# A two-layer audio transformer on one core: norm scaling on GpSimd and ScalarE, a spread-out order in the experts, and a split maximum in the second attention

## The chip, the cores and the metric

The kernel runs on one core of one Trainium2 chip. The metric is device time in microseconds, taken from the chip, of one execution of the whole program. TensorE, VectorE, ScalarE and GpSimd each run their own list of instructions and meet through semaphores; SyncE issues transfers.

## The reference, cut to what matters

A front end turns 16 signals into 16 sequences of 255 tokens with 64 features. Two layers follow, each an attention and a mixture of experts, all with a residual sum and a layer norm in front:

```python
def reference(x, ...):
    h = _L0_tok_ref(x)                                   # 16 x 255 x 64
    h = h + _L0_attn_ref(_layernorm(h), Q, K, VO)        # 8 heads, softmax over 255 keys
    h = h + _L0_ffn_ref(_layernorm(h), ...)              # 16 experts, 2 taken per token, a layer norm of its own
    h = h + _L1_attn_ref(_layernorm(h), ...)             # 8 heads, patch scores and position scores blended
    h = h + _L1_ffn_ref(_layernorm(h), ...)              # 8 experts
    return h

def _layernorm(x, eps=1e-05):
    m = mean(x); v = var(x)
    return (x - m) / sqrt(v + eps)

def _L0_ffn_ref(x, gate_w, gate_b, w1, b1, w2, b2, gamma, beta):
    topk_vals, topk_idx = top_k(x @ gate_w + gate_b, 2)
    topk_w = softmax(topk_vals)
    h = relu(einsum('bsh,ehf->bsef', x, w1) + b1)
    expert_out = einsum('bsef,efh->bseh', h, w2) + b2
    y = x + sum(topk_w * expert_out[topk_idx])
    return layernorm(y) * gamma + beta
```

## The kernel before, in words

**Layout.** Tokens lie 128 to a tile, two tiles to a sequence, 32 tiles of 128 x 64 in `res`, the residual. `x2` holds each normed tile twice side by side, so that its transposes fill 128 rows. The phases run one after the other: front end, first attention (`attention0`, about 127 to 389 us), first experts (`experts0`, 389 to 609), a short preparation, second attention (`attention1`, 644 to 850), second experts to 950. Within a phase the engines' orders are written out by hand; a block of each engine's code calls `slot` or `chunk` in step with the others. `link` waits on VectorE for its own last result.

**Layer norm (`TileNorm`, L500 to L540).** VectorE takes `bn_stats` (L515), `bn_aggr` (L521) and variance plus epsilon (L523). GpSimd raises it to −0.5 (`root`, L528). VectorE subtracts the mean and multiplies (`normed`, L531), `scale_twice` for each tile of a group, writing it twice.

**First attention.** A slot is a quarter of a two-sequence round (two heads pairs), so a sequence has two slots `g`. TensorE: projections (L612, L616), scores L624, the turn of the probabilities L634, outputs' turn L639, outputs L651. VectorE: maxima L787 of the scores, reciprocal L793, copy L799 of the turned probabilities, the residual sum L804, then statistics of the sequence before and, in the other slot, `scale_twice` for the sequence before that. ScalarE: exponentials L722, projections out L714, outputs out L730. GpSimd: weighing L872 (the exponentials times the reciprocals, two per slot), `fetch` L868 of the sequence two ahead between them, and `root`.

**First experts.** Eight chunks of 4 tiles; a chunk has 8 steps `e` of two experts each. TensorE per step: `hidden` L1616 of the next step, `second` L1624 of this one; in steps set by constants also the logits of the next chunk (L1598), the turned columns (L1590), the turned weights (L1606) and the turned sum of the chunk before (L1632). ScalarE: the relu L1695 (two per step), and in single steps `gap` L1679 (the exponential of the difference of the two best logits), the weights out L1685 and columns out L1675. VectorE: per step `scalar_tensor_tensor` L1823 (bias, times the spread weight) and a sum L1801; beside them `best` of the next chunk (L1722 to L1734: bias, `max`, `max_index`, the subtraction L1733, the cast), `places`, `shares` and `spread` (L1739 to L1756), and for the chunk before `finish` (L1765 to L1793: sum, own norm, gain, shift, residual) and `next_norm` (L1760) of the chunk before that. SyncE writes the weights to DRAM (L1891) and reads them back spread over the partitions (L1898), 2 x 4 per chunk. GpSimd: a fetch L1856 and two roots per chunk. The order is set by two places, the constants and the list of what VectorE does in each step:

```python
TURN_SUM, COLUMNS, LOGITS, WEIGHTS = 2, 6, 0, 4
...
extra = [first, ahead[0:2], ahead[2:3] + late[0:1], late[1:3], before[0:2], before[2:3], late[3:5], late[5:7]]
```

**Second attention.** Four units `p` per sequence. TensorE keeps operands in three bf16 parts: `project` L1251, `stack` L1257 gathers them with selector matrices, scores L1263, transposes L1297 of the maximum (as two bf16 parts `mhl`), turned scores L1269, outputs L1279 and the tail of the sequence before (L1312, L1319, L1323). ScalarE: stacks out L1358 and L1360, `high` L1366, outputs L1382, L1387, exponential L1393. VectorE: `maxima` L1418 to L1427 (the reduce L1420, its high part L1426, its remainder L1427), the sum `qm` L1438, the subtraction `remains` L1416 of the projected values in unit p = 0, statistics, `scale_twice`, blends L1450 to L1459. GpSimd: two further parts of the values (L1491, L1493), the pads L1500, the position scores' sum L1505. `stack` at p = 2 waits for those parts of the next sequence (`s_parts`).

## Time and profile before

| | |
|---|---|
| time, median of 3 runs | 949.48 us (949.08 to 949.72) |
| the profiled execution's own time | 951.54 us |
| its span, first to last instruction | 949.7 us |
| mean granted TensorE clock | 0.889 |
| TensorE busy | 696.9 us (73%) |
| VectorE busy | 673.8 us (71%) |
| ScalarE busy | 471.6 us (50%) |
| GpSimd busy | 307.3 us (32%) |

A row of the profile names line, engine and operation, then output and input by name, and how often it ran; behind the bar stand busy time, mean ns of one, and the idle time of the engine just before those instructions with what ended it. PE is TensorE, DVE VectorE, ACT ScalarE, POOL GpSimd, SP SyncE. PEclk, in stretches of the span, is the granted TensorE clock with 1.00 for 2.4 GHz and 0.50 for 1.2 GHz. The profiled execution is a little longer than the median of the runs (951.54 against 949.48 us).

### The profile page before, as it was taken

How to read it: one execution, taken by the hardware profiler on the slowest of the kernel's cores; microseconds unless marked ns; L12 is line 12 of the kernel's file. 1: busy time of each engine (PE TensorE's matmuls, PEld its weight loads, DVE VectorE, ACT ScalarE, POOL GpSimd, SP SyncE). 2: the span in 40 equal slices, each digit the busy share in tenths (PEclk: the TensorE clock that was granted, in tenths of full speed). 3: DMA queues.
4: the chain of work that ended last, by engine and by line, in shares of the span. 5: the costliest groups of instructions: out<-in, count | busy, mean ns of one | idle time of the engine just before them, and what ended most of it. 6: DMA issues, size and time to landing. Idle time of an engine off the chain costs nothing. (4 is left out here: it accounts for less than half of the span.)

```text
span 949.7 us, 16815 instructions
## 1 busy us (share of the span) xinstructions
PE 696.9 (73%) x5015; PEld 379.5 (40%) x5035; DVE 673.8 (71%) x1733; ACT 471.6 (50%) x1173; POOL 307.3 (32%) x310
## 2 busy tenths in 40 slices
PE   0012247899999998499988888376988888867895
PEld 0011124556565565222332322363554444546342
DVE  0289947888888888468777779764788888856353
ACT  0036437767667665055444444133766666632442
POOL 0299325555665656200111001242222222230000
PEclk9996558999999999699887889587999999985798
DMA  0200200000000000143222222000000000000000
GB/s 9 78 0 0 88 1 1 1 1 0 0 0 0 0 0 1 68 134 103 80 80 78 78 80 89 1 1 1 2 1 0 0 0 0 0 1 0 5 19 22
DMA packets 21240, 24.30 MB, mean 26 GB/s; under 512 B 11854, under 2 KB 12110, under 8 KB 20942
## 3 DMA queue, kind: packets, MB, share of 16 engines
q1 hardware_dynamic: 18989, 23.31, 8.1%
q10 hardware_dynamic: 2209, 0.49, 0.2%
q8 instruction: 19, 0.31, 0.1%
q14 instruction: 23, 0.19, 0.1%
HBM read 22.48 MB, written 1.31 MB: 25 GB/s over the span
## 5 line engine op out<-in xcount | busy, mean ns | idle before, releaser
L872 POOL TENSOR_TENSOR big<-big 128x1024 f32<-128x1024 f32 x64 | 121.1, 1893 | 72.2 <-DVE big L793 72.1
L722 ACT ACTIVATE big<-ps,big 128x255 f32<-128x255 f32 x256 | 117.6, 487 | 12.4 <-DVE big L787 7.0
L1695 ACT ACTIVATE big<-ps,b1s 128x512 f32<-128x512 f32 x128 | 80.1, 684 | 61.3 <-PE ps L1616 61.3
L528 POOL TENSOR_TENSOR big<-big 128x2 f32<-128x2 f32 (+1 forms) x48 | 39.5, 826 | 212.0 <-DVE big L523 212.0
L787 DVE TENSOR_REDUCE big<-ps 128x4 f32<-128x1020 f32 x64 | 74.7, 1209 | 23.4 <-PE ps L624 23.4
L799 DVE COPY mid<-ps 128x1024 f32<-128x1024 f32 x64 | 78.2, 1222 | 16.3 <-PE ps L634 10.8
L1624 PE MATMUL ps<-big,w2s 128*64 128x512 f32 x256 | 75.2, 668 | 16.3 <-ACT big L1695 16.2
L1420 DVE TENSOR_REDUCE big<-ps 128x4 f32<-128x1020 f32 x65 | 79.1, 1217 | 7.7 <-PE ps L1263 6.7
L1393 ACT ACTIVATE big<-ps 128x1024 f32<-128x1024 f32 x64 | 66.2, 1034 | 35.0 <-PE ps L1269 35.0
L634 PE MATMUL ps<-cst,big 128*128 128x128 f32 x512 | 67.6, 275 | 19.7 <-DVE mid L799 19.5
L1616 PE MATMUL ps<-big,wall 64*128 64x512 f32 x256 | 81.5, 707 | 0.0
L1823 DVE SCALAR_TENSOR_TENSOR big<-ps,b2s,mid 128x512 f32<-128x512 f32 x64 | 48.0, 751 | 43.0 <-PE ps L1624 21.7
L714 ACT ACTIVATE big<-ps 128x512 f32<-128x512 f32 x64 | 39.4, 616 | 70.9 <-PE ps L612 43.5
L634 PEld LDWEIGHTS ps<-cst,big 128*128 128x128 f32 x512 | 55.8, 141 | 37.7 <-issue 36.3
L651 PE MATMUL ps<-mid,big 128*64 128x256 f32 (+1 forms) x512 | 69.5, 392 | 0.3 <-DVE mid L799 0.3
L1257 PE MATMUL ps<-big,selqk 128*128 128x256 bf16 x396 | 57.2, 283 | 3.5 <-POOL big L1493 2.4
L722 ACT ACTIVATION_READ_ACCUMULATOR big<-ps,big 128x1 f32 x256 | 56.4, 220 | 0.0
L361 PE MATMUL ps<-cst,big 128*128 128x128 f32 x16 | 3.6, 386 | 66.8 <-DVE big L293 66.8
L387 PE MATMUL ps<-cst,big 128*128 128x128 f32 x64 | 15.1, 387 | 49.5 <-DVE big L445 32.9
L531 DVE TENSOR_SCALAR big<-res,big (+1 forms) x64 | 41.7, 693 | 4.8 <-POOL big L528 3.3
L1157 DVE TENSOR_TENSOR big<-big,ps 128x512 f32<-128x512 f32 x32 | 20.6, 684 | 32.6 <-PE ps L1066 21.9
L1257 PEld LDWEIGHTS ps<-big,selqk 128*128 128x128 bf16 x396 | 34.2, 100 | 22.0 <-issue 13.9
(251 smaller groups left out, 1400.1 us busy)
## 6 DMA issues: line engine op xcount, KB each, us to landing
mid<-spread_w SPq DMA_DIRECT2D x128, 128.0 KB, 2.8
mid<-in_split_sel SPq DMA_DIRECT2D x1, 1536.0 KB, 6.1
wall<-in_w SPq DMA_DIRECT2D x1, 1280.0 KB, 7.0
cst<-in_consts SPq DMA_DIRECT2D x1, 666.5 KB, 5.0
mid<-in_w_raw SPq DMA_DIRECT2D x1, 620.0 KB, 6.4
w2s<-in_w SPq DMA_DIRECT2D x1, 512.0 KB, 3.4
out_tokens<-res SPq DMA_DIRECT2D x8, 64.0 KB
out_tokens<-res SPq DMA_DIRECT2D x8, 63.5 KB
```

The costliest lines, as they stand in the source:

```text
L634: last = nc.tensor.transpose(AT[:, j, c, P * tq:P * tq + P], e_sb[r % 4][:, j, tq, P * c:P * c + P], ident)
L651: last = nc.tensor.matmul(O[D * j:D * j + D, par], val[par][0:n, c, D * h:D * h + D], a_sb[r % 4][0:n, j, c], start=(g == 0 and a == 0 and ...
L722: last = nc.scalar.activation(e_sb[r % 4][:, jj, tq, 0:NW], S[:, 2 * (r % 2) + jj, tq, 0:NW], ACT.Exp, scale=-1.0, bias=minus[r % 4][:, jj ...
L787: nc.vector.tensor_reduce(minus[r % 4], S[:, 2 * a:2 * a + 2, :, 0:NW], AX.X, ALU.min).then_inc(s_mx, 1)
L799: nc.vector.tensor_copy(a_sb[r % 4], AT).then_inc(s_at, 1)
L872: nc.gpsimd.tensor_tensor(e_sb[r % 4], e_sb[r % 4], bc(inverse[r % 4].unsqueeze(3), [P, 2, 2, 256]), ALU.mult).then_inc(s_A, 1)
L1257: last = nc.tensor.matmul(out_, selqk[:, 2 * p + n, part], parts[par][:, part], start=(part == 0), stop=(part == 2))
L1393: nc.scalar.activation(e_sb[k % 4], T, ACT.Exp, scale=scale).then_inc(s_E, 1)
L1420: link(nc.vector.tensor_reduce(mx, S[:, :, :, 0:NW], AX.X, ALU.max))
L1616: last = nc.tensor.matmul(H1(e, j), wst[0][half, f:f + P], xc[q][half], start=True, stop=True)
L1624: last = nc.tensor.matmul(Y(e)[D * j:D * j + D], w2s[0][:, 2 * e + j], hid[e % 2][j], start=True, stop=True)
L1695: last = nc.scalar.activation(hid[e % 2][j], H1(e, j), ACT.Relu, bias=b1s[0][:, 2 * e + j:2 * e + j + 1])
```

## The change

It has three parts. In the first attention VectorE's `scale_twice` goes, and GpSimd does the scaling in `normalise`: root, a wait for it, two `tensor_scalar` of 128 x 128. GpSimd's order becomes weigh, weigh, fetch or normalise, with its loop written out.

In the first experts the scalings of the own norm (four of 128 x 64, steps 4 and 5) and of the next one (four of 128 x 128, steps 1 and 2, for the chunk three before) are activations on ScalarE with a scale and a bias; GpSimd makes the bias, minus mean times root, in `root_and_shift`, behind waits of its own. The tile `new` and its sum go. `gap` moves from step 1 to step 3, the turned weights from 4 to 5, the turned sum from 2 to 1; the subtraction stands ahead of `max_index`, which with the cast becomes `which`, two steps later.

In the second attention TensorE's scores of the next unit wait for the reduce alone (`s_max`), the max transposes come behind scores, stack and the turned scores of the unit before, and the exponential one unit later. `mx` is double, VectorE's order is maxima, qm, `max_parts`, and `remains` and the statistics go from p = 0 to p = 1. OT moves to another bank of PSUM.

```diff
+            def root_and_shift(self, pool, i):
+
+                pool.wait_ge(self.s_var, i + 1)
+                nc.gpsimd.tensor_tensor(self.rs, self.var, self.nh, ALU.pow).then_inc(self.s_half_way, 1)
+                pool.wait_ge(self.s_half_way, 2 * i + 1)
+                nc.gpsimd.tensor_tensor(self.shift, self.both[:, :, 0], self.rs, ALU.mult).then_inc(self.s_half_way, 1)
+                pool.wait_ge(self.s_half_way, 2 * i + 2)
+                nc.gpsimd.tensor_tensor(self.shift, self.minus, self.shift, ALU.subtract).then_inc(self.s_rs, 1)
 
...
+                            if not known or b >= 2:
+                                dve.wait_ge(s_nx, b - 1)
                             norm.variance()
-                        if g == 0 and (not known or b >= 2):
-                            tiles = span(2 * (b - 2), 2)
-                            norm.scale_twice(dve, b - 2, x2[:, tiles], res[:, tiles])
                         copy(2 * k + 1, 2 * N + 1)
                         if unit:
                             inverses(2 * k + 3, 2 * N + 3)
...
-                    def slot(j, k, more=True):
-                        N = 2 * QUADS * j + k
-                        par, g = at(k)
-                        b = 2 * j + par
-                        weigh(2 * k, 2 * N)
-                        if g == 0 and more:
-                            fetch(b + 2, par)
-                        weigh(2 * k + 1, 2 * N + 1)
-                        if g == 1 and (not isinstance(j, int) or b >= 1):
-                            norm.root(pool, b - 1)
+                    def normalise(b):
+
+                        norm.root(pool, b)
+                        pool.wait_ge(norm.s_rs, b + 1)
+                        for n in range(2):
+                            t = 2 * b + n
+                            last = nc.gpsimd.tensor_scalar(x2[:, t], bc(res[:, t].unsqueeze(1), [P, 2, D]), norm.both[:, n, 0:1], norm.rs[:, n:n + 1],
+                                                           ALU.subtract, ALU.mult)
+                        last.then_inc(s_nx, 1)
 
                     for b in range(2):
                         fetch(b, b)
                     pool.wait_ge(norm.s_nh, 1)
                     pool.wait_ge(s_pad, 4)
-                    for k in range(2 * QUADS):
-                        slot(0, k)
-                    with pool.Fori(1, B // 2 - 1) as j:
-                        for k in range(2 * QUADS):
-                            slot(j, k)
-                    for k in range(2 * QUADS):
-                        slot(B // 2 - 1, k, False)
-                    norm.root(pool, B - 1)
+                    for b in range(B):
+                        for g in range(QUADS):
+                            for R in (4 * b + 2 * g, 4 * b + 2 * g + 1):
+                                weigh(R, R)
+                            if g == 0 and b + 2 < B:
+                                fetch(b + 2, b % 2)
+                            if g == 1 and b >= 1:
+                                normalise(b - 1)
+                    normalise(B - 1)
...
 
 
                         U = 2 * PAIRS * j + k
@@ -1288,20 +1301,23 @@
                         par, p = at(k)
                         b = 2 * j + par
                         if "unit" in do:
-                            pe.wait_ge(s_mhl, U + 1)
-                            if not known or U >= 1:
-                                pe.wait_ge(s_qm, U)
-                            if p == 0 and (not known or b >= 2):
-                                pe.wait_ge(s_otr, b - 1)
-                            for tq in range(2):
-                                last = nc.tensor.transpose(MT[:, P * tq:P * tq + P], mhl[k % 2][:, tq], ident_b[:])
-                            last.then_inc(s_mtp, 1)
                             pe.wait_ge(s_q, U + 2)
                             pe.wait_ge(s_k, U + 2)
+                            pe.wait_ge(s_max, U + 1)
                             scores(k + 1)
                             if p == 2:
                                 pe.wait_ge(s_parts, b + 2)
                             stack(at(k + 2)[0], at(k + 2)[1])
+                        if "turned" in do and (not known or U >= 1):
+                            pe.wait_ge(s_qm, U)
+                            if not known or U >= 2:
+                                pe.wait_ge(s_E, U - 1)
+                            turned_scores(k - 1)
+                        if "unit" in do:
+                            pe.wait_ge(s_mhl, U + 1)
+                            for tq in range(2):
+                                last = nc.tensor.transpose(MT[:, P * tq:P * tq + P], mhl[k % 2][:, tq], ident_b[:])
...
+                            if p == 3 and (not known or b >= 2):
+                                pe.wait_ge(s_oT, b - 1)
+                                nc.tensor.matmul(Y.rearrange("p t d -> p (t d)"), oT_sb, wps[:], start=True, stop=True).then_inc(s_y, 1)
                             if p == 3 and (not known or 1 <= b <= B):
-                                if "unit" in do:
-                                    pe.wait_ge(s_qm, U + 1)
                                 pe.wait_ge(s_O, QUADS * b)
                                 for tq in range(2):
                                     for g in range(QUADS):
                                         last = nc.tensor.matmul(OT[:, tq, 4 * HS * g:4 * HS * g + 4 * HS], o_sb[(par + 1) % 2][:, g, P * tq:P * tq + P], cmp, start=True, stop=True)
                                 last.then_inc(s_OT, 1)
...
                         if p % 2 == 0 and (not known or b >= 1) and "o" in do:
                             g = p // 2
                             act.wait_ge(s_PV, QUADS * b - 1 + g)
                             if g == 0 and (not known or b >= 3):
                                 act.wait_ge(s_OT, b - 2)
                             nc.scalar.activation(o_sb[(par + 1) % 2][:, g], O[:, g], ACT.Copy).then_inc(s_O, 1)
+                        if "exp" in do and (not known or U >= 1):
+                            act.wait_ge(s_T, U)
+                            if not known or U >= 5:
...
                         dve.wait_ge(s_S, U + 1)
-                        link(nc.vector.tensor_reduce(mx, S[:, :, :, 0:NW], AX.X, ALU.max))
+                        nc.vector.tensor_reduce(mx[k % 2], S[:, :, :, 0:NW], AX.X, ALU.max).then_inc(s_max, 1)
+
+                    def max_parts(U, k):
+                        dve.wait_ge(s_max, U + 1)
                         if not isinstance(U, int) or U >= 2:
                             dve.wait_ge(s_mtp, U - 1)
 
                         m = mhl[k % 2].rearrange("p t (j c) -> p t j c", j=2)[:, :, :, ROWS:ROWS + 2]
-                        mt = mx.rearrange("p j t -> p t j")
...
                         if "unit" in do:
+                            maxima(U + 1, k + 1)
                             dve.wait_ge(s_mtp, U + 1)
                             if not known or U >= 2:
                                 dve.wait_ge(s_T, U - 1)
                             nc.vector.tensor_tensor(qm[k % 2], qs[k % 4], MT, ALU.add).then_inc(s_qm, 1)
-                            maxima(U + 1, k + 1)
-                        if p == 0 and "unit" in do:
+                            max_parts(U + 1, k + 1)
...
+            TURN_SUM, COLUMNS, LOGITS, GAP, WEIGHTS = 1, 6, 0, 3, 5
             pos = [0]
             def take(n, dt=F32):
                 a = big[:, pos[0]:pos[0] + n]
@@ -1556,8 +1568,7 @@
+                    def own_scale(c, tiles):
+                        act.wait_ge(own.s_rs, c + 1)
+                        for t in tiles:
+                            nc.scalar.activation(yy[:, t], yy[:, t], ACT.Identity, scale=own.rs[:, t:t + 1], bias=own.shift[:, t:t + 1]).then_inc(s_sc, 1)
+
+                    def next_scale(c, tiles):
+                        act.wait_ge(norm.s_rs, c + 1)
+                        for t in tiles:
+                            one = slice(TC * c + t, TC * c + t + 1)
+                            nc.scalar.activation(x2[:, one], bc(res[:, one].unsqueeze(2), [P, 1, 2, D]), ACT.Identity,
+                                                 scale=norm.rs[:, t:t + 1], bias=norm.shift[:, t:t + 1]).then_inc(s_nx, 1)
...
-                            if e == LOGITS + 1 and (not known or c < CH - 1):
+                            if e in (1, 2) and c >= 3:
+                                next_scale(c - 3, ((0, 1), (2, 3))[e - 1])
+                            if e == GAP and c < CH - 1:
                                 gap(c + 1)
+                            if e in (4, 5) and c >= 1:
+                                own_scale(c - 1, ((0, 1), (2, 3))[e - 4])
...
-
                         for n in range(TC):
                             last = nc.vector.max(v8[:, n], lg[:, n])
                         link(last)
-                        nc.vector.memset(step[:, 1:2], 0.0)
+                        nc.vector.tensor_tensor(wts[:, 0], v8[:, :, 1], v8[:, :, 0], ALU.subtract).then_inc(s_dv, 1)
+
+                    def which(c):
                         for n in range(TC):
                             last = nc.vector.max_index(i8[:, n], v8[:, n], lg[:, n])
                         link(last)
-                        nc.vector.tensor_tensor(wts[:, 0], v8[:, :, 1], v8[:, :, 0], ALU.subtract).then_inc(s_dv, 1)
                         link(nc.vector.tensor_copy(idx, i8[:, :, 0:2]))
...
                     def next_norm(c):
 
-                        return [lambda: norm.stats(new), norm.variance,
-                                lambda: norm.scale_twice(dve, c, x2[:, span(TC * c, TC)], new)]
+                        def variance():
+                            if c >= 1:
+                                dve.wait_ge(norm.s_rs, c)
+                            norm.variance()
+
+                        return [lambda: norm.stats(res[:, TC * c:TC * c + TC]), variance]
...
-                        def scale():
-                            dve.wait_ge(own.s_rs, c + 1)
-                            for t in range(TC):
-                                last = own.normed(yy[:, t], yy[:, t], t)
-                            link(last)
-
                         def gain():
+                            dve.wait_ge(s_sc, TC * (c + 1))
                             link(nc.vector.tensor_tensor(yy, yy, bc(gb[:, 0].unsqueeze(1), shape), ALU.mult))
 
                         def shift():
                             link(nc.vector.tensor_tensor(yy, yy, bc(gb[:, 1].unsqueeze(1), shape), ALU.add))
 
                         def add():
-                            link(nc.vector.tensor_tensor(new, res[:, tl], yy, ALU.add))
                             nc.vector.tensor_tensor(res[:, tl], res[:, tl], yy, ALU.add).then_inc(s_fin, 1)
                             dve.wait_ge(s_fin, c + 1)
 
-                        return [total, stats, own.variance, scale, gain, shift, add]
...
-                        first = [lambda: best(c + 1)] if not known or c < CH - 1 else none
-                        ahead = combine(c + 1) if not known or c < CH - 1 else none * 3
-                        before = next_norm(c - 2) if not known or c >= 2 else none * 3
-                        extra = [first, ahead[0:2], ahead[2:3] + late[0:1], late[1:3], before[0:2], before[2:3], late[3:5], late[5:7]]
+                        total, stats, variance, gain, shift, add = finish(c - 1) if c >= 1 else [lambda: None] * 6
+                        places, shares, spread = combine(c + 1) if c < CH - 1 else [lambda: None] * 3
+                        next_stats, next_variance = next_norm(c - 2) if c >= 2 else [lambda: None] * 2
+                        first, second = [lambda: best(c + 1), lambda: which(c + 1)] if c < CH - 1 else [lambda: None] * 2
+                        extra = [[first], [total, stats], [variance, second], [places], [shares, spread], [next_stats, next_variance], [gain, shift], [add]]
...
+                    def chunk(c):
+                        if c < CH - 2:
                             fetch(c + 2)
-                        if not known or c >= 2:
-                            norm.root(pool, c - 2)
-                        if not known or c >= 1:
-                            own.root(pool, c - 1)
+                        if c >= 1:
+                            own_root(c - 1)
+                        if c >= 2:
+                            next_root(c - 2)
 
```

## Rows read from the trace of the kernel before

**Rows 1.** Waits of 389 to 609 us (us in total, times, longest).

```profile
PE ps L1624 <- ACT big L1695: 16.2, 8, 3.5
```

**Rows 2.** Timeline, TensorE (start, duration; idle before in brackets).

```profile
411.23 1.08 PE L1624 MATMUL ps<-big,w2s 128*64 128x512 f32 x4 [1.14 <-ACT big L1695]
...
451.81 1.76 PE L1624 MATMUL ps<-big,w2s 128*64 128x512 f32 x4 [1.91 <-ACT big L1695]
```

**Rows 3.** Timeline, first experts, around 477 us.

```profile
476.73 0.21 ACT L1679 ACTIVATE big<-big 128x4 f32<-128x4 f32 x1 [5.75 <-DVE big L1733]
...
477.00 0.75 DVE L1823 SCALAR_TENSOR_TENSOR big<-ps,b2s,mid 128x512 f32<-128x512 f32 x1 [0.22 <-DVE big L1734]
...
478.59 0.16 DVE L1751 TENSOR_TENSOR big<-big 128x4 f32<-128x4 f32 x1
```

**Rows 4.** Windows, TensorE (length, busy, count, PEclk, DMA share, GB/s).

```profile
404.99:588.69 183.70, 167.50 (x665) 0.90 0.30 93
412.00:414.00 2.00, 2.00 (x10) 1.00 0.55 199
452.00:454.00 2.00, 2.00 (x7) 0.52 0.36 93
```

**Rows 5.** Waits, TensorE, 252.98 to 267.62 us: one sequence.

```profile
PE ps L634 <- DVE mid L799: 1.0, 2, 0.7
```

**Rows 6.** Timeline, first attention.

```profile
251.72 0.69 POOL L528 TENSOR_TENSOR big<-big 128x2 f32<-128x2 f32 x1 [2.81 <-DVE big L523]
...
252.38 1.89 POOL L872 TENSOR_TENSOR big<-big 128x1024 f32<-128x1024 f32 x1
...
254.72 1.04 PE L634 MATMUL ps<-cst,big 128*128 128x128 f32 x8
...
257.75 2.32 DVE L531 TENSOR_SCALAR big<-res,big  x2
...
259.83 1.15 PE L624 MATMUL ps<-big 32*128 32x256 f32 x16
...
261.51 1.19 DVE L787 TENSOR_REDUCE big<-ps 128x4 f32<-128x1020 f32 x1
```

**Rows 7.** Timeline, second attention, VectorE.

```profile
742.47 0.60 DVE L531 TENSOR_SCALAR big<-res,big  x2
```

**Rows 8.** Window of one sequence of the second attention, TensorE.

```profile
738.10:749.88 11.78, 10.30 (x112) 1.00 0.00 0
```

**Rows 9.** Waits of 644 to 850 us.

```profile
PE ps L1297 <- DVE big L1427: 23.1, 46, 1.7
```

**Rows 10.** Groups by line and shape, GpSimd, whole span.

```profile
L528 POOL TENSOR_TENSOR big<-big 128x4 f32<-128x4 f32 x16 | 17.0, 1074 | 160.5 <-DVE big L523 160.5
...
L345 POOL TENSOR_SCALAR mid<-cst,posw,small 128x512 f32<-128x512 f32 x8 | 9.1, 1142 | 0.8
...
L1505 POOL TENSOR_TENSOR big<-big,mid 128x128 f32<-128x128 f32 x16 | 7.2, 453 | 82.8 <-DVE big L1454 82.8
```

**Rows 11.** Groups by line and shape, ScalarE, 389 to 609 us.

```profile
L1695 ACT ACTIVATE big<-ps,b1s 128x512 f32<-128x512 f32 x128 | 80.1, 684 | 61.3 <-PE ps L1616 61.3
...
L1679 ACT ACTIVATE big<-big 128x4 f32<-128x4 f32 x8 | 1.7, 206 | 36.6 <-DVE big L1733 36.6
```

**Rows 12.** Timeline, first experts, VectorE.

```profile
488.47 0.68 DVE L1801 TENSOR_TENSOR big<-big 128x512 f32<-128x512 f32 x1
```

**Rows 13.** Timeline, second attention, around 750 us.

```profile
748.87 0.42 DVE L1416 TENSOR_TENSOR big<-ps,big 128x256 f32<-128x256 f32 x1 [0.24 <-ACT big L1366]
...
749.46 0.61 POOL L1491 TENSOR_TENSOR big<-big 128x256 bf16<-128x256 f32 x1 [3.16 <-DVE big L1416]
...
750.15 0.67 POOL L1493 TENSOR_TENSOR big<-big 128x256 bf16<-128x256 f32 x1
...
751.75 0.18 DVE L1427 TENSOR_TENSOR big<-big 128x4 bf16<-128x4 f32 x1
...
752.53 0.72 PE L1257 MATMUL ps<-big,selqk 128*128 128x256 bf16 x5
```

125 lines of the change are left out of this document (59 added, 66 removed).

## The prediction

> **What bounds the kernel now.** I read the page first, then its TensorE clock line, then the waits and the timeline of each of the three stages that are edited. The three have different limits, so the shares of the whole span decide nothing.
>
> In the first experts stage TensorE is the longest engine, and it is held in one place per chunk: L1624 waits for ScalarE's L1695, 16.2 us in 8 waits, the longest 3.5 us [rows 1]. The stalls come once per chunk and grow, 1.14 us in the first, 1.91 in the third [rows 2]. The reader should ask what held L1695. ScalarE stood 5.75 us at L1679 (the exponential of the gap) for L1733 [rows 3], and the L1695 queued behind it ran only then. L1733 comes behind four `max_index`, which it does not need. What follows a stall costs again: from the first L1624 to the last the mean granted clock is 0.90 over 183.7 us, 1.00 behind the stall of 1.14 us and 0.52 (the 1.2 GHz level) behind that of 1.91 us [rows 4].
>
> In the first attention TensorE waits only 1.0 us of a sequence of 14.64 us, all of it at L634 for VectorE's copies [rows 5]. The two L531 are what VectorE has in excess: 2.32 us for two instructions, started at 257.75 [rows 6]. In the second attention the same pair takes 0.60 us [rows 7].
>
> In the second attention a sequence takes 11.78 us with TensorE busy for 10.30 of it [rows 8]. TensorE's one common wait is L1297 for L1427, 23.1 us in 46 waits [rows 9], nearly all of the 1.48 us.
>
> **First attention, L531 to GpSimd.** VectorE loses the pair, and the copy behind it can start sooner; but the maxima L787 behind that, at 261.51, read the scores L624, which end at 259.83 + 1.15 = 260.98 [rows 6]. So of 2.32 us only 261.51 − 261.03, about 0.46, come off. The price is on GpSimd: root at 251.72 (0.69), the next L872 at 252.38 [rows 6]. Now two `tensor_scalar` of 128x128 stand in front of that L872. Bounds for one: 0.45 (L1505, a `tensor_tensor` of the same shape, two inputs) and 1.14 (L345, a `tensor_scalar` of four times the size) [rows 10]. I take 0.45, the same size. With a wait of 0.05 the weighing ends 0.95 us later than its 254.27. TensorE's turn of it began at 254.72 [rows 6], 0.35 us more than it needed with 0.1 for the signal, so it is 0.6 us later; 0.3 of that TensorE waited behind it anyway. So a sequence gains 0.46 and loses 0.3: −0.15 us, times 14, **−2 us**. At 0.35 each it is −5, at 0.6 each +3. The regular stretch alone is touched by this; the fetch behind both L872 is covered (the sequence it fetches for is two later).
>
> The trace has the pair at 0.60 us on VectorE when it is undisturbed [rows 7]. The Trainium skill, "GPSIMD Engine Reference", section 8, speaks against the move: for elementwise work VectorE is structurally about twice as fast. By it, as an estimate, the pair would cost 1.2 us on GpSimd and this stage +3 instead of −2.
>
> **First experts: TensorE's part.** Gone is the wait of ScalarE for L1733: the subtraction now stands ahead of the `max_index`, and the exponential comes two steps later. So the 16.2 us of stalls go, and with them the slow clock: a mean clock of 0.90 between levels of 1.0 and 0.5 means a fifth of 183.7 us at the lower one, and half of those 36.7 us lost, 18.4 us. What is left is 183.7 − 16.2 − 18.4 = 149 us of work for 64 steps.
>
> **What takes their place.** (1) ScalarE now scales the chunk before: four 128x64 in steps 4 and 5, and four 128x128 in steps 1 and 2. One lies between 0.21 (L1679, 4 columns) and 0.68 (L1695, 512 columns) [rows 11]; nearer to the small one by size, with a scale and a bias read from memory: 0.40 and 0.45. ScalarE has the room: 3.4 us per chunk are added, and it stood 5.75 at L1679 alone. But the first scaling waits for GpSimd: power 1.07 (L528 on 128x4 [rows 10]), then a product and a difference of 128x4 that have no row. Bounds: 0.1 (0.45 for 32 times the columns, L1505) and 1.07 (the power itself); I take 0.30, as plain arithmetic. That chain starts when VectorE has the variance in step 2 and ends 2.0 us later, so the first L1695 of step 5 starts late, behind two scalings: TensorE's second product of step 5 waits **0.9 us**. (2) VectorE's work from step 2 to the sum of the weights: three times L1823 and L1801 (0.75 and 0.68 [rows 3, 12]), variance 0.6, `max_index` and cast 0.9, places 0.5, shares 0.6 (three like L1751's 0.16 [rows 3], spaced by 0.2), spread 0.75, gaps 0.3: 7.9 us. TensorE does three steps of 2.1 us and the wait of (1) in 7.1 us, so the turn of the weights (moved from step 4 to step 5) waits **0.9 us** for the rest. Both in each of 7 chunks: +13 us. (3) The scattered weights leave one step later, which takes 2.1 us from the spread's lead before the next chunk's L1823 needs it; by the timeline it has 3.4, so nothing. GpSimd's fetch comes first in its chunk and has most of a chunk in hand: nothing.
>
> 149 + 13 = 162 instead of 183.7: −21. Waits of 0.9 us are below the 1.14 us behind which the clock stayed at 1.00 [rows 4], so I count no slow clock. Behind the last step the eight scalings run on ScalarE beside VectorE instead of on it, and `new` is gone: −2. **−23 us** in all.
>
> **Second attention.** Scores wait for L1420 alone, and the transposes L1297 come behind scores, stack and turned scores: the 1.48 us per sequence go. But `remains` moves one unit later, behind the next L1420, L1438 and L1427. Today: L1416 at 748.87, L1491 at 749.46 (0.61), L1493 at 750.15 (0.67), so the parts are there at 750.82, and TensorE's stack asks for them at 752.53: 1.7 us in hand [rows 13]. Moved behind L1427, which ends at 751.93 [rows 13], L1416 runs from 752.1 and the parts are there 1.95 later, at 754.1; TensorE, without half of its waits by then, asks at 752.8 and waits 1.3 us. With three waits of up to 0.25 us for exponentials and for k that become visible, 0.54 together as I estimate, 1.84 us of waits stand against 1.48: +0.36 times 16 is +5.8, and the pipeline is one unit deeper at its start and end, +1.2. **+7 us**. Without the wait for the parts a sequence would be 10.8 us.
>
> **Sum.** −2 − 23 + 7 = −18 against the profiled execution's 951.54, 933.5. The median of the runs is 2.06 us below the profiled execution, so **931.5 us**. A measurement of this kernel tells about 0.2% from no change, 1.9 us.
>
> **Rivals.** *Slow clock stays* (0.20): the stage's clock fell behind a stall of 1.91 us; two waits of 0.9 us only 1.9 us apart may do the same. Then of the 18 us some 12 are not won, or a little more: 943 to 946. For it: they lie close together, and twice a chunk. Against: the first chunk's single wait of 1.14 us left the clock at 1.00 [rows 2, 4]. *The parts are in time* (0.10): if VectorE is further ahead than I have it, the second attention's sequence falls towards 10.8, −13 instead of +7: 911 to 915. *Slower* (0.07): GpSimd's small operations cost as the power, 1.07 each. The chain is then 1.6 us longer, ScalarE holds step 5's L1695 for 2.4 us per chunk; 7 × (2.4 + 0.9) = 23, and the clock drops behind each as now (18): 149 + 23 + 18 = 190 against 183.7; with +7 of the second attention, −2 of the first and −2 of the tail, 949.5 + 6 + 3 = 959. It decides from about 0.6 us per operation, where the wait passes 1.5 us and nears the 1.91 us behind which the clock fell: 149 + 7 × 2.4 + 18 = 184, and the sum is 953. *The change does not do what it says* (0.05): ScalarE's wait for the gap was only the releaser that came last, and behind it stands L1616 or the DMA; then the stage stands still and 947 to 951 come out. The forecast as summed: 0.58.
>
> **Numbers.** Likeliest 931.5; its own bounds (first attention −5 to +3, scaling costs, second attention +3 to +9) give 925 to 938. To hold the slow clock too the range goes up to 946, and down to 920 for half of the second attention's gain. Faster 0.88, same 0.05, slower 0.07.
>
> **What would show it.** Right: no wait of L1679 for L1733, L1624's waits for L1695 below 1 us, clock near 1.00 in the first experts stage, its steps' stretch near 162 us; L1257's wait for L1493 in each sequence of the second attention, some 1.3 us. Wrong: a clock still near 0.9 there; GpSimd's `tensor_scalar` far from 0.45; a second attention sequence below 11.8 us.

## The result, and the profile after

The changed kernel takes 942.01 us (median of 5 runs, 940.87 to 942.56) against 949.72 beside it (5 runs, 949.08 to 953.25): a ratio of 0.9905, 95% interval 0.9885 to 0.9925. That is 7.7 us less, where 18 were forecast. Its profiled execution has a span of 940.7 us at a mean clock of 0.903.

The stages follow one another, so each can be measured by itself, from its first TensorE instruction to the next stage's first, in the two profiled executions; the last row runs to the start of TensorE's last instruction:

| stage | before, us | after, us | moved | forecast |
|---|---|---|---|---|
| first attention | 262.3 | 270.7 | +8.4 | −2 |
| first experts | 220.7 | 195.9 | −24.8 | −23 |
| preparation | 34.2 | 34.0 | −0.2 | 0 |
| second attention | 206.6 | 215.2 | +8.6 | +7 |
| last preparation and experts | 89.4 | 88.1 | −1.3 | 0 |

Two stages did what was forecast, one went the other way. Groups of the changed kernel (page), with the waits in front of them; L646 is the turn of the probabilities (L634 before), L1635 `second` (L1624, [rows 1]), L1270 `stack` (L1257):

```profile
L646 PE MATMUL ps<-cst,big 128*128 128x128 f32 x512 | 69.3, 279 | 25.9 <-POOL big L882 16.2
...
L1270 PE MATMUL ps<-big,selqk 128*128 128x256 bf16 x396 | 58.0, 285 | 24.1 <-POOL big L1507 23.1
...
L1635 PE MATMUL ps<-big,w2s 128*64 128x512 f32 x256 | 69.1, 618 | 7.6 <-ACT big L1718 7.6
```

L1635's waits are down from 16.2 to 7.6 us. New are waits for GpSimd: L646 for the weighing L882, and L1270 for the second of the parts, L1507 (20.7 us in 16 waits; one wait of 2.4 us at the stage's start was there before).

**First experts.** The window over the steps, to be read against the first of [rows 4], and one chunk on the timeline (ScalarE's own scaling L1701, TensorE's L1635 of step 5, the turn of the weights L1617):

```profile
413.70:575.60 161.90, 152.15 (x670) 1.00 0.32 106
```

```profile
465.73 0.77 ACT L1701 ACTIVATE big<-big 128x64 f32<-128x64 f32 x2 [1.96 <-POOL big L540]
...
467.70 1.08 PE L1635 MATMUL ps<-big,w2s 128*64 128x512 f32 x4 [1.10 <-ACT big L1718]
...
468.99 0.60 PE L1617 MATMUL ps<-cst,big 128*16 128x128 f32 x4 [0.21 <-DVE big L1783]
```

161.9 us for the steps where 162 were forecast, at a clock of 1.00. ScalarE waits 1.96 us for GpSimd's L540, TensorE then 1.10 us for ScalarE (forecast 0.9) and 0.21 for the weights (forecast 0.9). What GpSimd's operations took there (groups by line and shape, 400 to 610 us):

```profile
L536 POOL TENSOR_TENSOR big<-big 128x4 f32<-128x4 f32 x16 | 16.1, 1009 | 120.8 <-DVE big L526 120.8
...
L540 POOL TENSOR_TENSOR big<-big 128x4 f32<-128x4 f32 x16 | 7.3, 457 | 1.3
L538 POOL TENSOR_TENSOR big<-big 128x4 f32<-128x4 f32 x16 | 4.5, 278 | 1.3
```

The power took 1.01 us, product and difference 0.28 and 0.46 on average (0.30 each was the forecast). In the chain that the own scaling waits for, the product took 0.20 and the difference 0.71: 0.91 where 0.60 was forecast.

**First attention.** GpSimd by line and shape, then one sequence on the timeline, [rows 6] before:

```profile
L890 POOL TENSOR_SCALAR big<-res,big 128x128 f32<-128x128 f32 x32 | 25.2, 795 | 1.7
```

```profile
254.45 0.72 POOL L531 TENSOR_TENSOR big<-big 128x2 f32<-128x2 f32 x1 [3.64 <-DVE big L526]
...
255.27 1.57 POOL L890 TENSOR_SCALAR big<-res,big 128x128 f32<-128x128 f32 x2
...
256.81 3.74 POOL L882 TENSOR_TENSOR big<-big 128x1024 f32<-128x1024 f32 x2
...
258.76 1.09 PE L646 MATMUL ps<-cst,big 128*128 128x128 f32 x8 [1.14 <-POOL big L882]
```

One `tensor_scalar` takes 0.80 us. The pair ends at 256.84, and only then the weighing runs whose reciprocal was there at 253.65; TensorE's turn of it waits 1.14 us. The root L531 comes every 15.09 us where it came every 14.64.

**Second attention.** TensorE at the `stack` of unit 2, twice, 12.11 us apart:

```profile
717.17 0.83 PE L1270 MATMUL ps<-big,selqk 128*128 128x256 bf16 x6 [1.30 <-POOL big L1507]
...
729.28 0.83 PE L1270 MATMUL ps<-big,selqk 128*128 128x256 bf16 x6 [1.30 <-POOL big L1507]
```

The wait for the parts is 1.30 us, as forecast (over the stage 1.1 to 1.3, once 2.0), and a sequence takes 12.11 and 12.19 us in turn, 12.15 on average, where it took 11.78 [rows 8].

### The profile page after: what moved, and what is told of

It is laid out like the page before. It is cut to its first block and busy times, and to the rows that moved or that the text cites. A ratio compares the mean times of both kernels' runs of the same rounds, so it can differ in the third digit from the quotient of the medians.

```text
span 940.7 us, 16398 instructions
## 1 busy us (share of the span) xinstructions
PE 684.3 (73%) x5015; PEld 375.4 (40%) x5035; DVE 622.0 (66%) x1617; ACT 490.3 (52%) x1237; POOL 342.6 (36%) x374
## 5 line engine op out<-in xcount | busy, mean ns | idle before, releaser
L882 POOL TENSOR_TENSOR big<-big 128x1024 f32<-128x1024 f32 x64 | 120.5, 1893 | 45.1 <-DVE big L805 45.1
L1429 DVE TENSOR_REDUCE big<-ps 128x4 f32<-128x1020 f32 x65 | 79.2, 1219 | 18.4 <-PE ps L1276 14.6
L646 PE MATMUL ps<-cst,big 128*128 128x128 f32 x512 | 69.3, 279 | 25.9 <-POOL big L882 16.2
L1270 PE MATMUL ps<-big,selqk 128*128 128x256 bf16 x396 | 58.0, 285 | 24.1 <-POOL big L1507 23.1
L646 PEld LDWEIGHTS ps<-cst,big 128*128 128x128 f32 x512 | 58.4, 143 | 42.1 <-POOL big L882 20.3
L1627 PE MATMUL ps<-big,wall 64*128 64x512 f32 x256 | 75.1, 655 | 0.0
L1635 PE MATMUL ps<-big,w2s 128*64 128x512 f32 x256 | 69.1, 618 | 7.6 <-ACT big L1718 7.6
L1367 ACT ACTIVATE big<-ps 128x256 bf16<-128x256 f32 x66 | 25.9, 392 | 81.8 <-PE ps L1270 81.7
L536 POOL TENSOR_TENSOR big<-big 128x4 f32<-128x4 f32 x16 | 16.1, 1009 | 120.8 <-DVE big L526 120.8
L1270 PEld LDWEIGHTS ps<-big,selqk 128*128 128x128 bf16 x396 | 34.5, 101 | 44.1 <-POOL big L1507 27.8
L531 POOL TENSOR_TENSOR big<-big 128x2 f32<-128x2 f32 x32 | 22.8, 713 | 60.7 <-DVE big L526 60.7
```

What stands on the lines that cost most here:

```text
L646: last = nc.tensor.transpose(AT[:, j, c, P * tq:P * tq + P], e_sb[r % 4][:, j, tq, P * c:P * c + P], ident)
L882: nc.gpsimd.tensor_tensor(e_sb[r % 4], e_sb[r % 4], bc(inverse[r % 4].unsqueeze(3), [P, 2, 2, 256]), ALU.mult).then_inc(s_A, 1)
L1270: last = nc.tensor.matmul(out_, selqk[:, 2 * p + n, part], parts[par][:, part], start=(part == 0), stop=(part == 2))
L1429: nc.vector.tensor_reduce(mx[k % 2], S[:, :, :, 0:NW], AX.X, ALU.max).then_inc(s_max, 1)
L1627: last = nc.tensor.matmul(H1(e, j), wst[0][half, f:f + P], xc[q][half], start=True, stop=True)
L1635: last = nc.tensor.matmul(Y(e)[D * j:D * j + D], w2s[0][:, 2 * e + j], hid[e % 2][j], start=True, stop=True)
```

## The experiments

**One stage undone.** `no_gpsimd_norm` is the changed kernel with the first attention of the kernel before, `no_split_max` with its second attention.

> The changed kernel with the first attention as it was before. By the two traces this stage, from its first projection to the first transpose of the experts, takes 262.3 us before and 270.7 after. Theory: the two tensor_scalar on GpSimd (0.80 us each, not the 0.45 forecast) hold the weighing and TensorE; undone, 8.4 us come back: 933.6, between 932.5 and 935. Rival: VectorE's relief is worth something at the other end of the stage (the experts' first steps begin with x2 ready earlier), so less comes back: 936 to 940.

Measured 934.49 us (933.69 to 934.89), ratio to before 0.9804 (0.9786 to 0.9822). The stage takes 262.6 us, 8.1 less than in the changed kernel, and the next ones are as there: 195.9 and 215.2 became 196.1 and 215.2. The theory's range held: the move to GpSimd costs what its stage shows, and nothing else depends on it.

> The changed kernel with the second attention as it was before. Stage before 238.7 us, after 246.9 (from its first projection to the second experts' first product). Theory: the wait for the remainders' parts (1.30 us in each sequence) costs more than the split maximum gives; undone, 8.2 us come back: 933.8, between 932.5 and 935. Rival: the stage's start and end are what is longer and lie beside other work: 937 to 940.

Measured 936.54 us (935.53 to 939.01), 0.9821 (0.9801 to 0.9841). The stage takes 207.6 us, 7.6 less, so the split maximum in this form costs nearly the 8.2 of the theory. The total lies 1.5 us above the theory's range and just below the rival's; in the profiled execution the last preparation took 34.6 us at a mean clock of 0.50, where the changed kernel's took 31.7 at 0.55.

**The remainders, ahead of the reduce.** `remainders_first`, on the changed kernel:

```diff
+                        if p == 1 and "unit" in do:
+                            remains(b + 1, (par + 1) % 2)
                         if "unit" in do:
                             maxima(U + 1, k + 1)
...
                             max_parts(U + 1, k + 1)
-                        if p == 1 and "unit" in do:
-                            remains(b + 1, (par + 1) % 2)
```

> The changed kernel, with VectorE's remains taken ahead of the reduce in unit 1 instead of behind qm and the maximum's parts; nothing else. It starts some 2.3 us sooner. Theory: TensorE's wait for GpSimd's parts (23.1 us in 17 waits) goes whole, and a sequence falls from 12.11 us to 10.8: 942 - 21 = 921; the reduce of that unit is 0.4 us later, which may give back up to 0.3 us in each sequence, so 920 to 927. Rival: TensorE then waits for the maximum or the exponentials instead, and the sequence stays between 11.6 and 12.1: 934 to 942.

Measured 929.20 us (928.03 to 930.12), 0.9745 (0.9725 to 0.9766). The stage falls from 215.2 to 202.2 us, below the 206.6 of before. Its waits, TensorE's and VectorE's (640 to 820 us):

```profile
PE ps L1276 <- DVE big L1429: 13.4, 28, 0.8
```

```profile
DVE big L1425 <- ACT big L1375: 17.5, 16, 1.2
```

Of the 23.1 us of waits for the parts only the 2.4 at the stage's start are left, and 13.4 us for the reduce L1429 have come: VectorE stands 17.5 us at L1425 (remains) for ScalarE's L1375 (`high`), with the reduce behind it. The theory's mechanism holds, its number was missed by 2 us: what is late next is `high`, which the change had put behind the exponential.

**The scalings back on VectorE, in the new order.** `scalings_on_vector`: the `normed` of before in step 3, `scale_twice` in step 6, roots without shift on GpSimd.

```diff
-extra = [..., [places], [shares, spread], [next_stats, next_variance], [gain, shift], [add]]
+extra = [..., [places, scale], [shares, spread], [next_stats, next_variance], [gain, next_scale], [shift, add]]
```

> The changed kernel, with the first experts' two scalings on VectorE as before, but in the new order (subtraction ahead of max_index, exponential in step 3, own scaling in step 3, next scaling in step 6). Theory: VectorE's work in a chunk is then about 23 us where TensorE's is 21, so each chunk takes 2 us more, and waits of that size bring the slow clock: 942 + 14 = 956 to 970. Rival: the new order alone, which frees ScalarE from waiting for max_index, was what gained, and the scalings could have stayed: 938 to 944.

Measured 955.32 us (954.23 to 961.28), 1.0042 (1.0018 to 1.0066): 0.4% above the kernel before, and just under the theory's 956. The ten runs lie at 954.2 to 955.6 (six) and at 960.0 to 961.3 (four), and the profiled one is of the upper group. In it the first experts take 211.5 us, 15.6 more than in the changed kernel. The window over the steps, then TensorE's waits:

```profile
412.20:590.00 177.80, 159.40 (x668) 0.95 0.31 96
```

```profile
PE ps L1617 <- DVE big L1775: 21.5, 8, 6.2
```

TensorE waits for the spread weights (21.5 us in 8 waits, 2.4 in a common chunk), and the clock is down to 0.95. In this order VectorE has to be relieved. It is one order alone: the own scaling stands in step 3, ahead of the work for the spread weights, and a version with both scalings behind it was not run.

**One line of it alone.** `subtract_alone`, on the kernel before: L1733 put ahead of the `max_index`.

```diff
                         link(last)
+                        nc.vector.tensor_tensor(wts[:, 0], v8[:, :, 1], v8[:, :, 0], ALU.subtract).then_inc(s_dv, 1)
                         nc.vector.memset(step[:, 1:2], 0.0)
                         for n in range(TC):
                             last = nc.vector.max_index(i8[:, n], v8[:, n], lg[:, n])
                         link(last)
-                        nc.vector.tensor_tensor(wts[:, 0], v8[:, :, 1], v8[:, :, 0], ALU.subtract).then_inc(s_dv, 1)
```

> The kernel before with one line moved: the subtraction L1733 ahead of the four max_index. Nothing else. The max_index take 0.7 us. Theory: ScalarE's exponential still waits in step 1, so the stalls of L1624 fall by 0.7 us each, from 3.5 to 2.8, and the clock still drops: 949.5 - 5 = 944.5, between 942 and 946. Rival (the subtraction's place is the whole matter): stalls below 1 us, clock 1.00 and 925 to 930.

Measured 940.96 us (937.63 to 943.51), 0.9894 (0.9846 to 0.9943): 11.8 us below the kernel before beside it for one line moved, where the theory gave 5; by the interval of the ratio it can be 5 to 15. The four runs are 937.6, 938.7, 943.3 and 943.5 us, and the profiled one is the shortest. In it the first experts took 207.2 us, 13.5 less than before. Two of its stalls, and the clock behind each of the two:

```profile
473.21 1.30 PE L1624 MATMUL ps<-big,w2s 128*64 128x512 f32 x4 [2.77 <-ACT big L1695]
...
499.18 1.08 PE L1624 MATMUL ps<-big,w2s 128*64 128x512 f32 x4 [3.15 <-ACT big L1695]
```

```profile
475.00:477.00 2.00, 2.00 (x9) 0.50 0.44 135
501.00:503.00 2.00, 2.00 (x11) 1.00 0.37 133
523.50:525.50 2.00, 2.00 (x10) 0.50 0.39 121
548.50:550.50 2.00, 2.00 (x11) 1.00 0.44 150
405.60:576.00 170.40, 157.52 (x668) 0.96 0.32 101
```

The stalls fell to 12.7 us in all (16.2 before), 3.5 less. The other part is the clock, 0.96 over the steps: it stood at 0.50 behind the stalls of 2.77 us (473) and 2.75 us (521), but at 1.00 behind those of 3.15 us (499) and 2.25 us (546). The theory took the clock to drop behind every one. In the kernel before it did so behind five of six (1.91, 3.50, 3.21, 2.71 and 2.98 us, not 1.14); four windows of 2 us from 480, 506, 533 and 559 us all have 0.50. As an estimate, at 1.00 − 0.96 = 0.04, twice that share of 170.4 us stood at the lower level and half of it was lost: 6.8 us, where the same working gave 18.4 for the kernel before.

**Three stages at once, first set.** `mixed_one`: in the first attention the root stays, and one `tensor_scalar` stands behind each weighing of the next slot; own scalings in steps 5 and 6; remains first and `high` ahead of the exponential.

```diff
                             for n in range(2):
                                 weigh(4 * b + 2 * g + n, 4 * b + 2 * g + n)
+                                if g == 0 and b >= 2:
+                                    scale(b - 2, n)
...
-                            if e in (4, 5) and c >= 1:
-                                own_scale(c - 1, ((0, 1), (2, 3))[e - 4])
+                            if e in (5, 6) and c >= 1:
+                                own_scale(c - 1, ((0, 1), (2, 3))[e - 5])
...
+                        if p == 0 and "unit" in do:
+                            high(b + 1, (par + 1) % 2)
                         if "exp" in do and (not known or U >= 1):
```

> The changed kernel with one edit in each stage; the stages run one after the other, so each is read by its own length (after: 270.7, 195.9 and 215.2 us for first attention, first experts with what follows to the next preparation, second attention). First attention: GpSimd's root stays behind the second weighing, but the two tensor_scalar of 0.80 us stand one behind each weighing of the next slot. Theory (it is their place ahead of the weighing, not their time, that costs): 255 to 258 us, below the 262.3 of before. Rival (GpSimd has no room for 1.6 us per sequence wherever they stand): 266 to 271. First experts: own scalings in steps 5 and 6 instead of 4 and 5. Theory: the wait of L1635 for ScalarE (7.6 us) goes, but the wait for the weights (L1617) grows by as much, since VectorE's chain to the spread is what ends next: 195 to 197. Rival: all of it is won: 189. Second attention: remains first and ScalarE's high ahead of the exponential in unit 0. Theory (remains waits 1.2 us for high and holds the reduce; that goes): 197 to 200 against 202.2 with remains first alone. Rival (the later exponential is what TensorE waits for next): 202 to 208.

Measured 912.52 us (911.37 to 914.70), 0.9587 (0.9543 to 0.9630). Stages: 257.5, 195.0 and 196.9 us; all three theories hold, two of them at the edge of their ranges. GpSimd in the first attention, with the same 0.80 us:

```profile
250.28 0.72 POOL L531 TENSOR_TENSOR big<-big 128x2 f32<-128x2 f32 x1 [3.64 <-DVE big L526]
250.97 1.90 POOL L882 TENSOR_TENSOR big<-big 128x1024 f32<-128x1024 f32 x1
252.85 0.80 POOL L888 TENSOR_SCALAR big<-res,big 128x128 f32<-128x128 f32 x1
253.61 1.90 POOL L882 TENSOR_TENSOR big<-big 128x1024 f32<-128x1024 f32 x1
255.49 0.79 POOL L888 TENSOR_SCALAR big<-res,big 128x128 f32<-128x128 f32 x1
```

and TensorE's waits in the first experts:

```profile
PE ps L1622 <- DVE big L1788: 9.2, 7, 1.4
...
PE ps L1640 <- ACT big L1723: 0.7, 2, 0.4
```

The weighing follows the root at once, and a sequence takes 14.21 us where it took 15.09. In the experts L1640 waits 0.7 us (7.6 in the changed kernel) and the turn of the weights L1622 9.2 (2.1, besides 5.9 at the stage's start): one wait took the other's place, and nothing is won.

**Three stages at once, second set.** `mixed_two`: the two scalings of the first attention left out altogether; one more power in the own norm's chain; remains between the reduce and qm.

```diff
-                        for n in range(2):
-                            t = 2 * b + n
-                            last = nc.gpsimd.tensor_scalar(x2[:, t], ...)
-                        last.then_inc(s_nx, 1)
+                        nc.gpsimd.memset(norm.shift, 0.0).then_inc(s_nx, 1)
...
+                        nc.gpsimd.tensor_tensor(own.shift, own.var, own.nh, ALU.pow).then_inc(s_more, 1)
+                        pool.wait_ge(s_more, c + 1)
                         own.root_and_shift(pool, c)
...
                             maxima(U + 1, k + 1)
+                            if p == 1:
+                                remains(b + 1, (par + 1) % 2)
                             dve.wait_ge(s_mtp, U + 1)
```

> The changed kernel with one edit in each stage, read by stage. First attention: GpSimd's two tensor_scalar are left out (so the first attention's output isn't normed again, x2 keeps old values), and nothing else is done in their place; behind the stage's last work GpSimd runs twelve probes: a tensor_scalar of 128x128 read twice from 64 columns with two pointers, one of 128x64 with two pointers, one of 128x128 with two constants, a tensor_tensor of 128x128. Theory: VectorE's relief is worth 0.46 us per sequence, so the stage takes 262.3 - 6.5 = 256, besides the probes' 5 to 8 us at its end; the pointers are what makes 0.80 us, and the one with constants takes 0.45. Rival: the read of the same columns twice is what costs, and the 128x64 one takes 0.3 or less. First experts: one power of 1.01 us more in the chain of the own norm. Theory (clock follows the length of the wait): L1635's waits grow from 1.1 to 2.1 us, the mean clock falls to about 0.9, and the steps' 161.9 us become 185 or more. Rival (the clock fell before for another reason): 161.9 + 7 = 169 and a clock of 1.00. Second attention: remains between the reduce and qm. Theory: no wait for the parts, reduce not held: 198 to 201. Rival: the parts are still 0.4 us late: 203 to 206.

Measured once, 926.99 us. The first attention took 263.1 us with the probes, within the theory's 256 and 5 to 8 for them. A sequence takes 14.21 us, to a hundredth the time of `mixed_one`: VectorE's relief is worth 14.64 − 14.21 = 0.43 us, and the scalings, well placed, cost nothing. The probes (groups by line and shape, GpSimd):

```profile
L904 POOL TENSOR_SCALAR big<-res,big 128x128 f32<-128x128 f32 x3 | 2.4, 798 | 0.0
L906 POOL TENSOR_SCALAR big<-res 128x128 f32<-128x128 f32 x3 | 1.9, 642 | 0.0
L905 POOL TENSOR_SCALAR big<-res,big 128x64 f32<-128x64 f32 x3 | 1.7, 578 | 0.0
...
L907 POOL TENSOR_TENSOR big<-res 128x128 f32<-128x128 f32 x3 | 1.4, 454 | 0.0
```

The `tensor_scalar` of 128x128 with pointers takes 0.80 us, with constants 0.64, of 128x64 with pointers 0.58, and the `tensor_tensor` 0.45. Neither theory holds: the pointers are 0.16 us of the difference, 64 columns 0.22, and with constants it is still 0.19 above the `tensor_tensor`.

In the first experts the waits and the clock are:

```profile
PE ps L1636 <- ACT big L1719: 11.7, 7, 1.7
```

```profile
407.00:577.00 170.00, 152.98 (x676) 0.99 0.32 101
```

The stage took 200.0 us, 4.1 more. The waits grew to 1.7 us only, 11.7 in all. The window runs 5 us past the last L1636; up to its end at 571.67 the steps took 164.6 us with the clock at 1.00. So the theory failed (185 or more, a clock of 0.9) and the rival's picture came, at a smaller size. As the waits stayed at 1.7 us and not 2.1, it is not shown what waits of 2.1 us would do. In the second attention the stage took 199.3 us, within the theory's range; TensorE still waits 5.9 us in 16 waits for the parts (L1271 for L1508), up to 0.5 each, so the rival's cause is there at a smaller size.

**The index earlier.** `index_earlier` is `mixed_one` with `which` in step 1:

```diff
-extra = [[first], [total, stats], [variance, second], [places], [shares, spread], ...]
+extra = [[first], [second, total, stats], [variance], [places], [shares, spread], ...]
```

> mixed_one with one edit more in the first experts: max_index and the cast stand in step 1 ahead of the sum, where VectorE waits (0.3 us for the sum, 1.1 in step 2), and no longer in step 2. Theory (the spread's chain on VectorE, 7.9 us from step 2, is what TensorE waits for, 9.2 us in 7 waits): 0.9 us leave it in each chunk, the waits fall to 3, and the stage from 194.9 to 189: 912.5 - 6 = 906.5, between 905 and 908.5. Rival (the sum and statistics behind it come late and hold something else, the accumulation or L1846): 910 to 913.

> index_earlier with the own scalings back in steps 4 and 5, as in the changed kernel. Theory (two waits in series, of which only the later one shows): with the chain to the spread short, the wait of L1635 for ScalarE of about 1.1 us per chunk is all visible again, as the variance is no later than before: 0.6 to 1.1 us per chunk more than index_earlier, 910 to 914. Rival (no matter where the scalings stand): the same as index_earlier within 1 us.

> The changed kernel itself, beside the two others. Both theories: 942 (940.9 to 943).

Measured 910.83 us (910.15 to 912.93), 910.79 (908.53 to 913.52) and 942.38 (941.87 to 943.71); ratios 0.9575 (0.9555 to 0.9594), 0.9574 (0.9554 to 0.9595) and 0.9903 (0.9886 to 0.9920). The first experts took 191.6 and 192.7 us, 3.3 and 2.2 less than in `mixed_one`, not 6: the first run missed the theory's range and lies in the rival's. Against the 912.5 of `mixed_one` the gain in the total is within the intervals. TensorE's waits, first of `index_earlier`, then with the own scalings early:

```profile
PE ps L1622 <- DVE big L1788: 12.1, 8, 5.9
```

```profile
PE ps L1622 <- DVE big L1788: 7.9, 7, 5.9
PE ps L1640 <- ACT big L1723: 5.0, 9, 0.6
```

Of 12.1 us, 5.9 lie at the stage's start, so 6.2 in seven chunks are left of 9.2. The statistics behind the index now end later, and VectorE's L1851 of step 2 waits for them (0.5 us in a chunk), which gives over half of the 0.9 us back. With the own scalings early, the waits split, 5.0 and 2.0, for nearly the same sum (6.9 and 7.0 us with the others): the second run's rival holds by the totals, though in the profiled executions its stage is 1.1 us longer. Either version is 4.3% below the kernel before and 3.3% below the changed one (910.8 / 942.4), the best that was run.

## Why the prediction was wrong, step by step

**The time.** 931.5 was forecast and 942.0 measured; the stages say where: the first experts and the second attention are within 2 us of their terms, and the first attention is 10 us from its own, nearly the whole miss.

**First attention: the step that failed is the price of GpSimd's `tensor_scalar`.** The prediction took 0.45 us, "the same size", from a `tensor_tensor` [rows 10]. The trace has 0.80. The gain was right: 0.46 forecast, 0.43 by `mixed_two`. The loss was forecast 0.3 and is 15.09 − 14.21 = 0.88; the two instructions are 0.70 us longer than taken, and in the changed kernel nearly all of that lies on TensorE's path. The upper bound named in the text, 1.14, held it, but the stage's range, +3, went only to 0.6 each (and by the text's own terms 0.6 gives 0.60 − 0.46 = 0.14, times 14, +2). With 0.80 put into the same sum, the loss is 0.3 + 0.69 = 0.99 and a sequence 0.53 longer, times 14: +7.4. So the mechanism was right, and the term that was mis-sized is this price, 0.45 for 0.80.

The 8.4 us are spread so, by the starts of the root L531 (L528 before): 0.8 ahead of the first, eleven spacings of 0.45 longer (4.9 in all), 0.9 in each of the two behind them, 0.9 behind the last. Part of this is the clock. Near the stage's end TensorE waits 1.9 us for the weighing; behind that wait its clock fell in the profiled execution, and did not in `after_same_chip`, the same kernel (in each fence a row of the timeline, then a window of 2 us with the clock):

```profile
379.27 1.62 PE L646 MATMUL ps<-cst,big 128*128 128x128 f32 x8 [1.89 <-POOL big L882]
...
381.00:383.00 2.00, 2.00 (x10) 0.50 0.00 0
```

```profile
378.81 1.09 PE L646 MATMUL ps<-cst,big 128*128 128x128 f32 x8 [1.90 <-POOL big L882]
...
381.00:383.00 2.00, 1.69 (x14) 1.00 0.00 0
```

There the stage took 269.0 us. In the three other kernels with this first attention it took 270.8 with the fall and 269.5 and 268.8 without, so the move costs 6.6 to 7.3 us without the fall and 8.4 with it.

The prediction also took the 2.32 us of VectorE's pair as they were and did not ask why they are not the 0.60 of [rows 7]. The first of the two ran beside GpSimd's weighing:

```profile
257.75 2.07 DVE L531 TENSOR_SCALAR big<-res,big  x1
...
257.84 1.89 POOL L872 TENSOR_TENSOR big<-big 128x1024 f32<-128x1024 f32 x1 [1.16 <-DVE big L793]
```

It took 2.07 us and ended 0.08 us behind the weighing, and the second took 0.34. This is so in all 14 sequences up to 376 us: one of the pair takes 1.85 to 2.07 us and ends 0.08 or 0.09 us behind L872. To leave the pair on VectorE, at a place with no weighing beside it, was not tried.

On the Trainium skill ("GPSIMD Engine Reference", section 8): its statement that VectorE is about twice as fast gave, as an estimate, 1.2 us for the pair, and had the right direction; the trace shows 1.59 us against 0.60 on VectorE [rows 7], 2.6 times as long.

What no price would have shown is that the place decides. `mixed_one` has the same 1.6 us on GpSimd and loses nothing, because they stand behind a weighing and not ahead of one that is already free to run.

**First experts: right, with a cause that was taken too plainly.** 161.9 us for the steps against 162, and the clock at 1.00. The first wait was 1.1 us for 0.9, the second 0.21 for 0.9; the waits were 3 us less than the 13 forecast and the work 3 us more than the 149 (TensorE was busy for 152.2), so that the two errors cancelled and the exact 162 is luck. That both were one slack seen twice was missed: `mixed_one` took the first away and the second grew by as much. The removed stall as a cause is borne out by `subtract_alone`, which wins 13.5 of the 24.8 us in its profiled execution; how the rest divides between the later exponential and the scalings' move is not shown. `scalings_on_vector` adds that with the scalings on VectorE at the places tried the new order is lost again. That the clock drops behind each stall of 1.9 us or more, which the rivals rested on, is not so: it fell behind 2.77 and 2.75 and not behind 3.15 and 2.25, and at 1.9 us it fell in one execution and not in another. What decides it stays open. The 18.4 us came from the mean clock, and with the clock at 1.00 over the steps they were won.

**Second attention: right, the sum in part by luck.** +8.6 for +7, the wait 1.30 us for 1.3, a regular sequence 12.15 us for 12.14. But by the spacings of VectorE's L1425 (L1416 before) the first four sequences are 5.3 us longer together and the other twelve 4.3, and the end gives 1.1 back, where the forecast had 5.8 evenly and 1.2 at the ends; what makes the first four longer was not tried. `remainders_first` shows the cause: with the remainders early the split maximum does gain. It reached 11.5 us per sequence; with `high` ahead of the exponential (`mixed_one`) 11.08 and 196.9 us for the stage, 9.7 below before. The 10.8 us that the prediction named was not reached.

**The rivals.** None of them came. The clock did not stay low (0.20), the parts weren't in time (0.10), GpSimd's small operations took 0.28 and 0.46 us, below the 0.6 from which that case would have decided (0.07); in the chain that counts, 0.20 and 0.71, which is 0.46 each on average. ScalarE's wait for the gap was the one that held the stage (0.05). The measured 942.0 lies near the slow clock's 943 to 946, but for another reason: over the steps the clock was at 1.00.

## What to carry to other kernels

Price an instruction by the same operation on the same engine, not by another of the same size; where there is no such row, carry the upper bound through to the range. A helper engine's extra work costs its place in the queue: put it behind the instruction that others wait for, and it may be free. When several waits follow one another in a loop, ask which chain ends next before counting them as a sum, and after a wait is moved look at what the moved instruction now waits for. When an instruction takes several times what it takes elsewhere, look at what the other engines ran beside it before you move it away.

## What the runs showed of the hardware that was not expected

On GpSimd a `tensor_scalar` of 128x128 f32 took 0.80 us with two pointers and 0.64 with two constants, a `tensor_tensor` of that shape 0.45. VectorE's `tensor_scalar` of 128x128 took 1.85 to 2.07 us beside GpSimd's `tensor_tensor` of 128x1024 (1.89 us), ending 0.08 or 0.09 us behind it, and 0.34 us otherwise. TensorE's granted clock fell to the 1.2 GHz level behind idle times of 2.77 and 2.75 us and stayed at the 2.4 GHz level behind 3.15 and 2.25 us, in one execution of one loop; behind a wait of 1.9 us at one place of one kernel it fell in one execution and not in another. On ScalarE a scaling with scale and bias read from memory took 0.43 us for 128x64 and 0.49 for 128x128.
